# Moving one batch's routing work by a tile, cutting a table in four, and dealing GpSimd's scatters out evenly

## What is computed

```python
x = x + 0.5 * ffn(layernorm(x))       # top 2 of 8 experts, 128 -> 512 -> 128, then a layer norm
x = x + attention(layernorm(x))       # per batch of 1024 rows:
#   diff = softmax(q1 k1^T * scale) - lam * softmax(q2 k2^T * scale);  out = rmsnorm(diff v) * 0.2
x = x + 0.5 * ffn(layernorm(x))       # the same experts, routed anew
```

## Time and profile before

| | |
|---|---|
| median of three runs | 646.53 us |
| the profiled execution | 645.7 us, with a span of 644.0 us |
| mean granted TensorE clock | 0.967 of full speed |
| attention of b = 2 | about 327 to 385 us of the span |
| attention of b = 3 | about 385 to 450 us |
| second feed-forward half | about 450 to 606 us, then the last sums |

### The profile page before, as it was taken

One profiled execution on the slowest core, in us unless ns is written; L12 is line 12 of the kernel. 1 busy time (PEld: TensorE's weight loads), 2 busy tenths in 40 slices (PEclk: granted clock), 3 DMA queues, 4 the chain that ended last, 5 costly groups with the idle time before them and its releaser, 6 DMA issues.

```text
span 644.0 us, 16630 instructions
## 1 busy us (share of the span) xinstructions
PE 583.0 (91%) x4382; PEld 537.3 (83%) x4382; DVE 452.1 (70%) x1421; ACT 446.4 (69%) x1224; POOL 386.9 (60%) x481
## 2 busy tenths in 40 slices
PE   5987999999999788899899899887999999999964
PEld 5887999999999577788797789777989999999831
DVE  5784788446685989699769968976537665467645
ACT  4755666676767577776887696685777777896644
POOL 3007565657667786668515386585775777765633
PEclk9588999999999999899999999999899999999979
DMA  8902233223324210000000001021341423531051
GB/s 259 329 8 58 76 77 71 79 75 89 83 65 80 57 29 17 17 25 18 10 1 0 2 30 36 10 71 31 88 103 57 103 76 97 204 96 40 29 196 66
DMA packets 41882, 45.97 MB, mean 71 GB/s; under 512 B 8726, under 2 KB 32706, under 8 KB 41536
## 3 DMA queue, kind: packets, MB, share of 16 engines
q1 hardware_dynamic: 32496, 27.13, 14.4%
q0 software_dynamic: 9088, 17.75, 10.1%
q10 hardware_dynamic: 208, 0.02, 0.0%
HBM read 25.95 MB, written 19.83 MB: 71 GB/s over the span
## 4 chain that ended last, share of the span: by engine, by line
PE 56%; DVE 20%; ACT 9%; issue 6%; POOL 6%; DMA 1%; ACTq 0%; DVEq 0%; SPq 0%; POOLq 0%
PE banks L1076 20%; PE banks L1086 19%; DVE nb L1841 6%; DVE scratch L1848 3%; PE banks L1069 3%; PE banks L1173 2%; PE banks L964 2%; PE banks L966 2%; PE banks L965 2%; DVE st_r L1338 1%; POOL rows L499 1%; POOL zb L512 1%; DVE mv L1344 1%; ACT tgt L650 1%; POOL rs L480 1%
## 5 line engine op out<-in xcount | busy, mean ns | idle before, releaser
L1076 PE MATMUL banks<-scratch 128*128 128x128 f32 x1248 | 169.1, 279 | 1.8 <-ACT scratch L707 1.3
L1086 PE MATMUL banks<-blocks,scratch 128*128 x1248 | 166.5, 276 | 2.0 <-issue 1.1
L1076 PEld LDWEIGHTS banks<-scratch 128*128 128x128 f32 x1248 | 154.5, 195 | 4.7 <-issue 4.4
L1591 DVE TENSOR_SCALAR scratch<-banks,blocks 128x128 f32<-128x128 f32 x312 | 95.1, 346 | 89.5 <-PE banks L1076 77.5
L1086 PEld LDWEIGHTS banks<-blocks,scratch 128*128 128x128 f32 x1248 | 151.8, 192 | 4.6 <-issue 4.2
L491 POOL DMA_INDIRECT scratch<-xrows,rowbuf x78 | 75.4, 966 | 81.8 <-DVE rowbuf L1486 41.2
L698 ACT ACTIVATE scratch<-banks 128x128 f32<-128x128 f32 x156 | 43.1, 277 | 89.4 <-PE banks L1069 86.9
L789 ACT ACTIVATE scratch<-banks,nb 128x1024 f32<-128x1024 f32 x64 | 71.3, 1115 | 47.6 <-DVE nb L1841 47.2
L524 POOL DMA_INDIRECT results<-scratch,places x78 | 77.8, 998 | 34.4 <-issue 19.7
L714 ACT ACTIVATE scratch<-banks,blocks 128x128 f32<-128x128 f32 x312 | 96.4, 364 | 2.4 <-PE banks L1076 2.1
L707 ACT ACTIVATE scratch<-blocks 128x512 f32 x156 | 97.0, 622 | 0.1
(11 more groups left out here) (265 smaller groups left out, 896.4 us busy)
## 6 DMA issues: line engine op xcount, KB each, us to landing
scratch<-rows SPq DMA_DIRECT2D x78, 64.5 KB, 1.9
yrows<-scratch SPq DMA_DIRECT2D x78, 64.0 KB, 1.5
scratch<-in_L_ffn_W_dram SPq DMA_DIRECT2D x1, 2048.0 KB, 19.8
xrows<-tgt SPq DMA_DIRECT2D x4, 512.0 KB, 4.2
x<-in_L_attn_x_dram SPq DMA_DIRECT2D x3, 512.0 KB, 8.0
scratch<-xrows,rowbuf POOLq DMA_INDIRECT x78, 2.6
results<-scratch,places POOLq DMA_INDIRECT x78, 2.4
rows<-padrows SPq DMA_DIRECT2D x18, 64.5 KB
```

Of the source, the lines that this page charges most:

```text
L1076: ins = pe.matmul(hT_at(T, c), staged(T, c), xT_of(T), start=True, stop=True)
L1086: ins = pe.matmul(y_at(T), hT_of(T, c), blocks[:, W2_AT + c * D:][:, bass.ds(at, D)], start=(c == 0), stop=(c == FC - 1))
L1591: ins = dve.tensor_scalar(hT_of(T, c), hT_at(T, c), blocks[:, B1_AT + c:][:, bass.ds(at, 1)], 0.0, ALU.add, ALU.max)
```

## The change

Four edits, all of them of places in the engines' loops. No instruction is added or taken away.

```diff
         def choose_tile(b):
-            return 0 if b == BATCHES - 1 else 3
+            return 0 if b == BATCHES - 1 else 4
         def place_tile(b):
-            return 2 if b == BATCHES - 1 else 5
+            return 2 if b == BATCHES - 1 else 6
...
# GpSimd
-                    if b == 2 and i >= 5:
-                        scatter(1, 0, (range(3), range(3, 7), range(7, 10))[i - 5])
-                    if b == 3 and i < 2:
-                        scatter(1, 0, (range(10, 14), range(14, PAIRS))[i])
-                    if b == 3 and 2 <= i < 6:
-                        scatter(1, 1, (range(2), range(2, 5), range(5, 9), range(9, 13))[i - 2])
-                    if b == 3 and i == TB - 1:
-                        scatter(1, 1, range(13, PAIRS))
+                    if b == 2 and i >= 6:
+                        scatter(1, 0, (range(2), range(2, 6))[i - 6])
+                    if b == 3 and i < 3:
+                        scatter(1, 0, (range(6, 10), range(10, 13), range(13, PAIRS))[i])
+                    if b == 3 and i >= 3:
+                        scatter(1, 1, (range(3), range(3, 7), range(7, 10), range(10, 13), range(13, PAIRS))[i - 3])
...
# TensorE
-                    if b > 1 and i == choose_tile(b) + 1:
-                        prefix(a - 1)
                     if 2 <= i < TB - 1:
                         turn(b, i - 2)
                     if 3 <= i < TB - 1:
                         values(b, i - 3)
+                    if b > 1 and i == choose_tile(b) + 1:
+                        prefix(a - 1)
...
# VectorE
+                tabling = table(0)
                 for i in range(TB):
...
-                    if b == BATCHES - 1 and i == 4:
-                        at_once(table(0))
+                    if b == BATCHES - 1 and i >= 4:
+                        at_once(itertools.islice(tabling, (2, 2, 1, 2)[i - 4]))
```

## The result

The changed kernel takes 648.12 us (median of 22 runs), the kernel before 646.57 in as many: 1.55 us more. The ratio is 1.0035, with a 95% interval of 1.0023 to 1.0047, so 1.5 to 3.0 us more.

The account below looks back on a forecast made before the run. The prediction took GpSimd's last scatter, which starts the second half, as the bound. Added pieces and strikes, +3.0 to 3.1 us, behind a 1.65 earlier start gave +1.4: median 646.53 to 648.0, 8-in-10 range 645.6 to 649.7.

Parts of the forecast that it names:

- What bounds: Start of the second half: set by GpSimd's last scatter landing and its load, with GpSimd full from b = 3's `rstd`.
- The other leg: `value_scale(3, 0)`, `add_values(3, 0)`, `choose`, `prefix(6)` and last `values`: shift by the same 1.4 us, staying just ahead of the load.
- The lead of b = 2: Handover from b = 2 to b = 3: later choose and place start b = 3 1.65 us earlier, bounds 0.7 and 2.2.
- Two more pieces: GpSimd's queue behind b = 3's `rstd`: 16 scatter pieces instead of 14, costing 2 x 1.27 = +2.5 us.
- The strikes: End of b = 3: GpSimd instructions starting under VectorE's `difference` are held until it ends; +0.5 us, bounds -2.5 and +0.9.
- The sum for the start: Start of the second half: +3.0 to 3.1 us behind a start 1.65 earlier, so +1.4 us.
- The table's cut: Table in four parts from b = 3's tile 4: worth 0, since GpSimd waits for no one.
- All later work hangs on these two legs: Second half: starts by the last piece's load or the leg through `choose`, so the whole +1.4 us reaches the time.
- The clock: TensorE's low clock near the second half's start: longer idle might add 0.2 to 0.5 us, kept for the range.
- No gain upstream: Rival: handover from b = 2 to b = 3 keeps its time, so +3.1 us, 649.6; chance 0.15.
- The strikes miss: Rival: GpSimd's pieces start ahead of the `difference` and are not held; about 646.5 us; chance 0.17.
- GpSimd not full: Rival: GpSimd's queue has 3.1 us idle after 416, the added pieces fill it; 644.9 us; chance 0.13.

Follow-up runs that it names:

- e1_tail: Changed kernel with the scatter pieces from b = 3's tile 0 on dealt as before, 14 behind `rstd` instead of 16; ratio to before 0.9992.
- e4_table: Changed kernel with the table built whole at tile 4 again instead of in four parts; ratio to before 1.0030.
- f2_warm: Changed kernel with 24 idle TensorE transposes ahead of the last turn and 24 ahead of `prefix(6)`; ratio to before 1.0020.
- f3_halves: Changed kernel with VectorE's `difference` of b = 3's tiles 4 to 7 split in two halves; ratio to before 1.0004.
- h1_swap: Changed kernel with the last `values` ahead of `prefix(6)` in TensorE's queue; ratio to before 1.0023.
- g2_values: g1_scale with the last `values` also put ahead of `prefix(6)` in TensorE's queue; ratio to before 0.9948, the best version found.
- f1_tail: The same kernel as e1_tail, run again for its time; ratio to before 0.9963.
- e3_tiles: Kernel before with batch 0's choose and place a tile later and the later prefix, 4 and 6 pieces at b = 2's tiles 6 and 7; ratio 1.0027.
- h2_tiles: The same kernel as e3_tiles, run again on a chip where before takes 646.8 us; ratio to before 0.9991.
- f4_early: Changed kernel with scatter pieces issued earlier, one ahead of `rstd`, so 12 stand behind it instead of 16; ratio to before 0.9972.
- g1_scale: f4_early with `value_scale(3, 0)` put ahead of tile 7's `ratio` instead of behind it; ratio to before 0.9976.
- e2_deal: Kernel before with only the changed kernel's new dealing of scatter pieces; ratio to before 1.0065.
- the first ten experiments: All follow-up kernels except h1_swap and h2_tiles, run on chips where the kernel before takes 773 to 778 us; times rough to about 0.3%.

## Why the prediction was right, and where it was off

The path up to the start of the second half was forecast in its parts, and the experiments bear it out. Behind the start it was not: that the shift of the start is the shift of the time was an assumption, and it doesn't hold.

- **What bounds.** Right for before and changed: the second slot tile is turned by GpSimd's last scatter. The turn comes 5.5 us behind the last piece in before, changed, e1_tail, e4_table, f2_warm, f3_halves and h1_swap (117.98 - 112.45 = 5.53, 119.87 - 114.37 = 5.50, 118.01 - 112.55 = 5.46, and so on), 5.9 in g2_values. The other leg came up where the last `values` took 3.1 us or more at the low clock: with an early last piece in f1_tail, e3_tiles, h2_tiles, f4_early and g1_scale, but in e2_deal too, whose last piece is the latest of all. One name was wrong: the turn at 450.62 is that of the second slot tile. The first ran at 449.42, behind the last `values`.
- **The lead of b = 2.** Forecast 1.65, measured 85.33 - 83.69 = 1.64, and 1.5 to 1.7 in all kernels with the later tiles. e3_tiles shows that it comes from them.
- **Two more pieces.** 2 x 1.27 = 2.5, as forecast; e1_tail against the changed kernel confirms it with what hangs on them.
- **The strikes.** Forecast +0.5. From the steps between ratios: tile 4 6.10 for 5.95, tiles 5 and 6 together 9.61 for 6.06, of which 2.53 are pieces, and `ratio(7)` 1.02 for 1.54. That is +0.15 + 1.02 - 0.52 = +0.65. f3_halves shows the mechanism. Each new strike costs 1.0 by these steps, as forecast.
- **Not foreseen: 0.39 us.** `rstd`'s end to `ratio(4)` took 4.24 in place of 3.85 for the same three pieces. The first piece starts 0.57 behind `rstd`, not 0.18. `scatter` puts its two waits ahead of a batch's first piece, and that piece has moved from tile 2, where GpSimd was waiting anyway, to tile 3 behind `rstd`. e2_deal and e4_table, with the new dealing, take 4.3 there as well, e1_tail, e3_tiles and f4_early 3.8. That both waits were already met is what the place in the program and the `<-issue` of that piece say; their price alone was not measured.
- **The sum for the start.** Forecast 3.05 - 1.65 = +1.4. Measured 2.53 + 0.65 + 0.39 = 3.57 (3.56 by the ends), less 1.64: +1.92 for the last piece, +1.89 for the turn. The terms mis-sized are the waits, taken as nothing (0.39), and the strikes (0.15). The parts add up too: e2_deal +2.86, e3_tiles -1.62, the table's cut +0.68, together +1.92.
- **The table's cut.** Off: I took 0, and with the new dealing it cost 0.68. The step that failed is that GpSimd waits for no one. It does not wait for the difference, but it is held by it, and the cut let the difference start ahead of a piece. The strike that I forecast at tile 4 came at its price, but it is the cut that brought it, not the dealing.
- **From the start to the end: luck.** The prediction says "All later work hangs on these two legs" and adds the whole shift of the start to the time. In the two profiled executions the shift doesn't stay what it was. The slot tiles' turns, and the end of the span, all from R:

| | 2nd | 4th | 10th | 40th | 58th | 78th, the last | end |
|---|---|---|---|---|---|---|---|
| before | 117.98 | 122.97 | 134.49 | 198.03 | 232.43 | 273.32 | 311.36 |
| changed | 119.87 | 123.41 | 135.35 | 198.62 | 233.56 | 274.46 | 312.87 |
| changed, later by | 1.89 | 0.44 | 0.86 | 0.59 | 1.13 | 1.14 | 1.51 |
| h1_swap | 119.86 | 123.40 | 135.84 | 199.14 | 234.68 | 275.58 | 313.82 |

So 1.45 us go within two tiles and most of that comes back later, by waits that the prediction doesn't have. That the medians moved by 1.55 where +1.4 was forecast is in part luck.
- **The clock.** Left out of the sum, and its sign in the range was wrong: it was to cost the changed kernel 0.2 to 0.5, and it gave back most of the shift. Granted clock from 450 to 458 us, of before and then of the changed kernel (from:to, us, busy of each engine, PEclk, DMA share, GB/s):

```profile
450.00:454.00 4.00, 3.38 (x15) 3.13 (x16) 0.61 (x2) 2.92 (x12) 3.15 (x6) 0.50 0.27 72
454.00:458.00 4.00, 4.00 (x35) 4.00 (x35) 2.56 (x10) 2.48 (x10) 3.08 (x4) 0.93 0.47 103
```

```profile
450.00:454.00 4.00, 2.29 (x15) 1.68 (x15) 1.21 (x6) 3.03 (x13) 2.69 (x5) 1.00 0.26 63
454.00:458.00 4.00, 4.00 (x39) 4.00 (x38) 2.96 (x12) 2.86 (x12) 2.88 (x3) 1.00 0.37 99
```

Before idled 2.27 us ahead of `prefix(6)`, and its low stretch covers the last `values` and the first slot tiles. The changed kernel idled 2.95 us ahead of the last `turn`; its low stretch came earlier, ended in the wait for `choose`, and its first slot tiles run at 2.4 GHz. From the second to the third turn it needs 1.42 us, before 2.30; e4_table and e2_deal, whose clock is low there too, need 2.29 and 2.45. One execution of each kernel was profiled, and e1_tail and f1_tail, the same kernel, have their low stretch in different places. So it isn't shown that the change moves it in every execution.
- **From the tenth tile on.** TensorE waits there for ScalarE in both, 0.40 ahead of the turn in the changed kernel and 0.34 behind it in before, and ScalarE stands behind GpSimd's next `rstd`. Its last instruction, in before and then in the changed kernel, ends 132.44 and 133.29 from R:

```profile
464.88 0.20 POOL L482 TENSOR_SCALAR nm<-nm 128x8 f32<-128x8 f32 x1
```

```profile
465.22 0.20 POOL L482 TENSOR_SCALAR nm<-nm 128x8 f32<-128x8 f32 x1
```

At the 56th tile TensorE waits once more in the changed kernel, 0.20 us, and not in before, for a load that took 8.14 us (from its chain):

```profile
553.30 8.14 DMA scratch<-rows
...
561.48 0.33 PE banks L1067
```

- **The rivals.** No gain upstream: refuted by e3_tiles and e2_deal. The strikes miss: three of three struck in the changed kernel; with the table whole (e2_deal, e4_table) tile 4's first piece got in ahead of the difference. GpSimd not full: no gap above 0.6 in the profile. The Trainium skill's port lock ("SBUF — State Buffer", "SBUF: two separate sides") agrees with the trace: each struck piece ended 0.94 behind the difference's end, so it waited out all of it. The price of 1.1 a strike, drawn from it, was a little high, since a first piece that nothing holds takes 1.07 and not 0.96.

Open: the changed kernel's runs spread from 646.1 to 651.9, nine of 22 at 649.3 or more, before's from 644.3 to 647.8. h1_swap's profiled execution (649.96 us) has the changed kernel's second and fourth turns and loses more behind them. At the tenth tile it is 0.49 later than the changed kernel, since its `prefix(6)` stands behind the last `values` and GpSimd waits 1.36 for batch 2's `place`. At the 56th its load makes TensorE wait 0.84 in place of 0.20, 0.6 more. So loads in the second half can cost one execution and not the other. Whether that makes the spread, and how much of the 1.55, stays open.

## What to carry to other kernels

Evening out an in-order queue is no gain by itself. What counts is how much of the work stands behind the last point at which the queue was still waiting, here GpSimd's `rstd`: look for that point, and move pieces ahead of it, not merely apart. When a stage is opened by two legs, shortening one shows little until the other is shortened too; ask at each step which wait ends last. And follow a shift past the start of the stage, with the granted clock beside it: here 1.89 us were 0.44 two tiles on. A forecast that meets the time has not thereby met the way to it.

## What the runs showed of the hardware

- VectorE's `difference` (128 x 1024 float32, both tiles in SBUF) holds up a GpSimd indirect DMA that is issued while it runs, by the whole rest of it: 2.09 us in place of 1.07 behind a 1.28 us difference, 1.56 behind the first of two of 0.7. A piece already under way when the difference starts is not slowed (1.07 in e4_table), nor is the difference (1.27). Delaying VectorE a little can therefore be worth more than letting it run early: in e4_table it was worth 0.68.
- The low clock falls on different work from one kernel to the next, and even between executions of one. The last `values` took 2.0 us at 2.4 GHz and up to 3.73 where the granted clock was 0.50 (e2_deal); f1_tail and e1_tail, the same kernel, had 3.47 and 2.02, and second turns 0.46 apart.
- The chips of the first ten experiments took 773 to 778 us for the kernel before. In f1_tail's timeline TensorE stands still in the first half like this, with nothing in the profile that it waits for in the first case:

```profile
168.49 2.07 PE L1086 MATMUL banks<-blocks,scratch 128*128 x8 [6.00 <-issue]
184.96 0.45 PE L1069 MATMUL banks<-ident,scratch 128*128 128x128 f32 x1 [14.40 <-ACT scratch L698]
```

From R to GpSimd's last piece the attention on the same chips kept its instants to about 0.1 us. What stops the expert halves there stays open.
